# Reordering the tensor-engine blocks of an up-and-down-sampling kernel: all up blocks of an image, then all down blocks

## The reference

```python
x = x + sin(einsum('oc,chw->ohw', W, coord) + b[:, None, None])[None]
out = x + bias[None, :, None, None]
out = sep_upfirdn(out, 2 * up_filter, up=2, down=1, pad=(6, 5))    # width, then height
out = leaky_relu(out, 0.2) * sqrt(2)
out = sep_upfirdn(out, down_filter, up=1, down=2, pad=(5, 5))
```

## Time and profile before

| | |
|---|---|
| median of 3 runs | 6847.44 us (6846.39 to 6847.5) |
| the profiled execution | 6846.66 us |
| its span, first to last instruction | 6844.9 us |
| PE busy (matmuls) | 6782.4 us, 99% |
| PE weight loads | 6303.4 us, 92% |
| ACT busy | 4084.0 us, 60% |
| DVE busy | 3954.3 us, 58% |
| POOL busy | 1296.0 us, 19% |
| HBM traffic | 558 MB, 82 GB/s |

### The profile page before, as it was taken

How to read it: one execution, slowest core, us unless ns; L and a number is a source line. 1 busy time by engine, 2 the same in 40 slices (tenths; PEclk the granted TensorE clock), 3 DMA queues, 4 the chain that set the end, 5 groups by cost and what they waited for, 6 DMA issues and landing times.

```text
span 6844.9 us, 361569 instructions
## 1 busy us (share of the span) xinstructions
PE 6782.4 (99%) x148480; PEld 6303.4 (92%) x148480; DVE 3954.3 (58%) x6218; ACT 4084.0 (60%) x7688; POOL 1296.0 (19%) x1041
## 2 busy tenths in 40 slices
PE   6999999999999999999999999999999999999999
PEld 6999999999999999999999999999999999999998
DVE  6555555555555555555555555555555555555555
ACT  4566566655666665566566656656665665666555
POOL 2111111111111111111111111111111111111111
PEclk9999999999999999999999999999999999999999
DMA  3222222222222222222222222222222222222222
GB/s 116 81 81 81 80 81 81 81 81 81 80 80 81 81 80 81 81 81 81 80 81 81 81 81 81 80 80 81 81 80 81 81 81 80 80 81 81 81 81 74
DMA packets 580065, 558.27 MB, mean 82 GB/s; under 512 B 40400, under 2 KB 574928, under 8 KB 580048
## 3 DMA queue, kind: packets, MB, share of 16 engines
q1 hardware_dynamic: 580048, 558.02, 25.8%
HBM read 278.94 MB, written 278.92 MB: 82 GB/s over the span
## 4 chain that ended last, share of the span: by engine, by line
PE 99%; DVE 1%; issue 0%; DMA 0%; ACT 0%; SPq 0%; DVEq 0%
PE y_ps L450 34%; PE p_ps L434 34%; PE o_ps L434 15%; PE a_ps L450 14%; PE o_ps L460 3%; DVE up_band L377 0%; DVE angle L354 0%; DVE angle L352 0%; DVE phase L344 0%; ACT trig L258 0%; DVE trig_parts L361 0%; DVE angle L356 0%; DVE turns L348 0%; DVE turns L350 0%; DVE trig_parts L360 0%
## 5 line engine op out<-in xcount | busy, mean ns | idle before, releaser
L392 DVE SCALAR_TENSOR_TENSOR z<-y_ps,leak 128x512 f32<-128x512 f32 x4096 | 2716.1, 684 | 1522.9 <-ACT leak L278 1522.9
L278 ACT ACTIVATE leak<-y_ps 128x512 f32<-128x512 f32 x4096 | 2245.3, 605 | 1024.0 <-PE y_ps L450 1024.0
L450 PE MATMUL y_ps<-up_band,a_sb 64*128 64x138 f32 (+2 forms) x32768 | 2807.5, 288 | 1.6 <-ACT a_sb L271 1.5
L434 PE MATMUL p_ps<-down_band,z 128*64 128x68 f32 (+1 forms) x65536 | 2445.9, 227 | 1.8 <-DVE z L392 1.0
L434 PEld LDWEIGHTS p_ps<-down_band,z 128*64 128x64 f32 x65536 | 2156.2, 137 | 267.3 <-DVE z L392 1.3
L450 PEld LDWEIGHTS y_ps<-up_band,a_sb 64*128 64x128 f32 x32768 | 2228.7, 186 | 148.7 <-issue 1.8
L245 POOL TENSOR_TENSOR x_sum<-x_raw,f_sb 128x512 f32<-128x512 f32 x1024 | 1283.6, 1281 | 5514.0 <-ACT f_sb L264 5504.6
L400 DVE COPY p_rows<-p_ps 128x512 f32<-128x512 f32 x2048 | 1411.0, 689 | 1350.4 <-PE p_ps L434 1277.0
L271 ACT COPY a_sb<-a_ps 128x512 f32<-128x512 f32 x2048 | 1100.3, 589 | 1179.8 <-PE a_ps L450 1179.8
L450 PE MATMUL a_ps<-up_band,x_sum 64*128 64x138 f32 (+2 forms) x16384 | 1297.0, 275 | 26.7 <-POOL x_sum L245 26.6
L434 PE MATMUL o_ps<-down_band,p_rows 128*64 128x68 f32 (+1 forms) x32768 | 1171.0, 224 | 0.7 <-issue 0.7
(11 more groups left out here) (28 smaller groups left out, 40.7 us busy)
## 6 DMA issues: line engine op xcount, KB each, us to landing
x_raw<-in_x_dram SPq DMA_DIRECT2D x1024, 256.0 KB, 2.7
out_dram<-o_out SPq DMA_DIRECT2D x1024, 256.0 KB, 2.1
f_rows<-trig_dram SPq DMA_DIRECT2D x512, 20.0 KB
trig_dram<-trig_parts SPq DMA_DIRECT2D x32, 256.0 KB, 2.5
trig_dram<-ones SPq DMA_DIRECT2D x4, 256.0 KB, 2.3
trig_dram<-bias_wide SPq DMA_DIRECT2D x4, 256.0 KB, 2.5
up_taps<-in_L_conv_up_filter_dram SPq DMA_DIRECT2D x1, 6.0 KB, 2.3
down_taps<-_L_conv_down_filter_dram SPq DMA_DIRECT2D x1, 6.0 KB, 2.4
```

Of the source, the lines that this page charges most:

```text
L278: nc.scalar.mul(leak[i % 2][:, :], y_ps[i][:, :], SLOPE * GAIN).then_inc(leak_done, 1)
L392: nc.vector.scalar_tensor_tensor(z[n][:, i, :], y_ps[i][:, :], GAIN, leak[i % 2][:, :], ALU.mult, ALU.max).then_inc(z_done, 1)
L434: last = nc.tensor.matmul(out_ps[half * HALF:(half + 1) * HALF, lo:hi], data[:, t, col:col + HALF], down_band[:, band:band + hi - lo], sta ...
L450: last = nc.tensor.matmul(outs[o][:, lo:hi], data[row, k, (at + o) * P:(at + o + 1) * P], up_band[row, band:band + hi - lo], start=step == ...
```

## The change

On PE the two column blocks of the second pair and the second row block move ahead of the sines and of the first half of rows down; columns down moves between the two halves of rows down. A slot on PE is then: five or six up blocks (pair 0 step 0, rows step 0, pair 0 step 1, pair 1 step 0, rows step 1, pair 1 step 1), [sines], rows down half 0, columns down, rows down half 1. On ACT, copy_a goes ahead of copy_f. On DVE, leaky 1 goes ahead of copy_p half 0, and leaky 2 and 3 ahead of copy_p half 1. Waits, buffers and matmuls are the same.

```diff
--- before.py
+++ after.py
@@ -289,10 +289,10 @@
                 if y:
                     leaky(m, 0)
                     leaky(m, 1)
+                if a_next:
+                    copy_a(m + 1, 1 - n)
                 if f_next and n == 0:
                     copy_f(c + 1)
-                if a_next:
-                    copy_a(m + 1, 1 - n)
                 if y:
                     leaky(m, 2)
                     leaky(m, 3)
@@ -403,15 +403,14 @@
                 m = 2 * c + n
                 if y:
                     leaky(m, n, 0)
+                    leaky(m, n, 1)
                 if p:
                     copy_p(m - 1, 1 - n, 0)
                 if y:
-                    leaky(m, n, 1)
+                    leaky(m, n, 2)
+                    leaky(m, n, 3)
                 if p:
                     copy_p(m - 1, 1 - n, 1)
-                if y:
-                    leaky(m, n, 2)
-                    leaky(m, n, 3)
 
             slot(0, 0, p=False)
             slot(0, 1)
@@ -505,20 +504,19 @@
                     up_rows(m + 1, 1 - n, 0)
                 if y:
                     up_cols(m, n, 0, 1)
+                    up_cols(m, n, 1, 0)
+                if a_next:
+                    up_rows(m + 1, 1 - n, 1)
+                if y:
+                    up_cols(m, n, 1, 1)
                 if f_next and n == 0:
                     sines(c + 1)
                 if p:
                     down_rows(m - 1, 1 - n, 0)
-                if y:
-                    up_cols(m, n, 1, 0)
-                if a_next:
-                    up_rows(m + 1, 1 - n, 1)
-                if y:
-                    up_cols(m, n, 1, 1)
+                if o:
+                    down_cols(m - 2, n, c + 2 if f_done is None else f_done)
                 if p:
                     down_rows(m - 1, 1 - n, 1)
-                if o:
-                    down_cols(m - 2, n, c + 2 if f_done is None else f_done)
 
             pe.wait_ge(bands_ready, 1)
             sines(0)
```

More of the change, by code:

```diff
@@ L517, in slot @@
                     up_cols(m, n, 1, 1)
+                if f_next and n == 0:
+                    sines(c + 1)
+                if p:
+                    down_rows(m - 1, 1 - n, 0)
+                if o:
+                    down_cols(m - 2, n, c + 2 if f_done is None else f_done)
                 if p:
                     down_rows(m - 1, 1 - n, 1)
-                if o:
-                    down_cols(m - 2, n, c + 2 if f_done is None else f_done)
             pe.wait_ge(bands_ready, 1)
```

## The result

The changed kernel takes 6572.9 us (median of 4 runs, 6572.6 to 6574.1) against 6846.9 us of the kernel before, run beside it: a ratio of 0.960 with a 95% interval of 0.9583 to 0.9617: 274 us less. The forecast was 6529, the range 6465 to 6590.

The account below looks back on a forecast made before the run. PE's own sequence was taken as the bound. Per image step -0.22 - 0.15 + 0.01 + 0.05 = -0.31 us; over 1023 steps -317, last stage -1, from 6846.7 to 6529 us; range 6465 to 6590.

Parts of the forecast that it names:

- Steps 1 and 2: PE: two shape changes removed per image, up to down -0.22 us, down to up -0.15, +0.01 back; sum -0.36.
- Rival C: PE: second pair's first column-up block is held until the block before is through, +0.35 us an image, 6888 us; chance 0.03.
- D: PE: the 0.22 and 0.15 us belong to something other than shape and come back elsewhere, 6898 us; chance 0.02.
- E: PE: down blocks' loads cannot run ahead into a down block's matmuls, so 0.15 us is not saved, 6682 us; chance 0.02.
- Step 3: PE: second rows-down half waits for DVE's copy of p_ps from the first half, 0.05 us on every image.
- Rival A: PE: the second rows-down half's wait is absorbed, saving 0.36 instead of 0.31 us an image, 6477 us; chance 0.09.
- Step 4: Even images: columns down overwrites o_ps after ACT's copy_f; expected in time, cost 0.
- rival B: ACT late with copy_f, so columns down comes 0.43 us late on even images, 6724 us; chance 0.08.
- step 5: ACT: copy_a moved ahead of copy_f, with a_sb and POOL's sum of x in time; cost 0.
- Step 6: ACT and DVE: leaky 2, z 2 and z 3 moved later, still ready for the next image's second pair; cost 0.

## Why the prediction was right, and by how much it missed

- The bound (PE's own sequence, no recurring wait) was right: every microsecond of the difference is found in load-to-load distances of PE.
- Steps 1 and 2, -0.36 us: right. C1 fell to 0.46, also with C2 right behind it, which no row had shown; D0 fell to 0.97. Read to the nanosecond the three terms make 0.367. That the tile shape and not the moving length makes the price is not shown (above), and the sum does not need it. Rival C, that C2 would be held, is out; so are D (6573 and not 6898, and six changes cost what the theory says) and E (O and D1 follow a down block at 0.97 where nothing is waited for).
- Step 3, D1's wait for the copy: the mechanism was right, and the size on odd images too (0.05). The step failed where it said "on every image": on even ones the wait is 0.14. The 1.25 us from load to copy was read off the wrong rows for them. The block that loads at 3008.36 is a D1, whose copy has one wait in the code, and the other is the last image's D0, outside the loop; the copy behind a D0 has two waits, and inside the loop of the kernel before the one for D0 stood on a register instruction on even images. (The gap of 7.22 to 7.28 in that step is 0.06 and not 0.05; the sum went by 1.99 - 1.94, which is 0.05, and holds.) The rows had the longer time: the D0 that loads at 3012.48 had its copy 1.33 us later, with DVE idle since 3013.66:

```profile
3013.81 0.69 DVE L400 COPY p_rows<-p_ps 128x512 f32<-128x512 f32 x1
```

- 510 x 0.088 = 45 us is the miss of 6573 - 6529 = 44. That the two agree so well is in part luck, since smaller errors cancel: C3 costs 0.688 and not 0.679 (9 us), D1 in last place 1.124 where O in last place cost 1.129 (-5), and the 0.367 was taken as 0.36 (-7). Rival A, that the wait would be absorbed, is out: the wait was paid in full.
- Step 4, copy_f in time for O: right. copy_a came 2.75 and copy_f 3.69 us after C0's load, against 2.75 and 3.71 in the forecast, and O followed D0 at 0.97; rival B is out. The order of copy_a and copy_f on ACT did not matter, as step 5 said: without the swap the time is the same.
- Step 6, z of banks 2 and 3 in time for C2: right, and it hangs on DVE's new order, by 0.69 us an image.
- What I said the profile would show was wrong in one point: the list of waits was to have PE on p_rows a thousand times for some 50 us. It has 2 times and 1.7 us, with 97 us paid. On the even step above, O's loads end at 3011.56 and D1's begin at 3011.61, so 0.05 us of the wait stands as idle time of the loads, too little to be in the list, and the matmul records, whose ends are modelled, leave no idle time at all.
- The rule quoted with rival E, of the Trainium skill, "TensorE: Matmul & The Clock Gate", Part 3, says that loads overlap matmuls in flight only in other array rows. The traces here disagree for these tiles: blocks that use all 128 rows follow each other at 0.97 us, with 32 loads listed at 0.137 us each, and O's first load starts 0.005 us ahead of the start of D0's last matmul (median of the changed kernel's trace). The same section of the Trainium skill also lets a load go ahead when it targets the background weight buffer; no trace here shows whether that is the case.

## What to carry to other kernels

Where PE is the bound and its tiles have more than one shape, price each block by the distance from its first load to the next block's, sort by the neighbour's shape, and group blocks of one shape; here a pair of changes cost 0.36 to 0.37 us, whatever stood at them. Then list, for each block that moved nearer to its predecessor, which PSUM bank it has to get back: a single bank between two neighbours cost 1.02 to 1.11 us, with one block between them 0.05 to 0.14. See to it that the instruction that does the work holds the semaphore that comes last, and look in the trace whether it does, in each unrolled copy of a loop body: the copies here were not built alike. And read a duration from the row of the same block, not from its neighbour's.

## What the runs showed that I had not expected

- A wait that ends on a register instruction ahead of the DVE copy cost 0.086 us more than the same wait on the copy itself (6572.9 and 6529.2 us, 510 times). The two written waits are given to instructions differently in two copies of the same source line.
- Waits of 0.05 to 0.14 us of PE, 97 us in all, leave no trace in its list of waits, nor in its busy share of 99%.
- The change costs more going from the up blocks' 64x128 tiles to the down blocks' 128x64 (0.22 us) than back (0.15 to 0.16), and the sines' 10-row tile between them adds 0.43 us for its two written matmuls in either place.
